# Second layer normalisation of a fused block moved from VectorE to ScalarE, its shift and the output's shift to GpSimd

## The chip, the cores and the metric

The kernel runs on one NeuronCore of a Trainium2 chip. The metric is the device time of one execution in microseconds, as a median over runs.

## What is computed

The input is `x` of 8 batches, 1024 rows and 512 columns in fp32. One block of attention kind and one feed-forward block follow each other, each inside two layer normalisations:

```python
x = x + _layernorm(attn(_layernorm(x)))
x = x + _layernorm(ffn(_layernorm(x)))

# attn(x): s = sigmoid(silu(x @ s_w1 + s_b1) @ s_w2.T + s_b2); u = (x @ B_w.T + B_b) * s
#   h_t = h_(t-1) @ A.T + u_t over the 1024 rows;  y = h @ C_w.T + C_b + x @ D_w.T + D_b
#   returns y * sigmoid(x @ g_w.T + g_b)
# ffn(x): sq_relu(x @ Ws1) @ Ws2 + a routed part, whose weight trunc(softmax(top2)) is 0
#   except where it is exactly 1
# _layernorm(x) = (x - mean) / sqrt(var + 1e-05) over the last axis
```

## The kernel before

A batch is 8 tiles (`L = 8`) of 128 rows, in two halves of `MS = 4`. TensorE does every product three times over (`mm3`, L416 to L418) with operands split in a high and a low part, since the high part alone would be too coarse. The order of the instructions of each engine is written out by hand, in two functions with the same names on each engine: `tail_and_scan` (the gates 0 to 3 of batch b and the 12 steps of its state scan, mixed with the end of batch b-1's feed-forward) and `body` (the rest of batch b up to its first half of the feed-forward, mixed with the first normalisation and projections of batch b+1). Batch 0 and batch 7 are written out, and batches 1 to 6 are six passes of one hardware loop on each engine. Engines wait for each other by counting semaphores alone, and each engine works through its queue in the order written.

The names that matter here, for tile `j`:

- `attn(j)`, `attn_norm(j)` on VectorE: product with the gate, its statistics, the normalisation. `x1(j)` on GpSimd (L1480) adds the input and gives `xres`, the input of the second block.
- `x1_stats(j)` on VectorE (L1039, L1040, L1095): mean and variance of `xres` in `mvx`, `rsx`. `x1_rs(j)` on GpSimd (L1456): `rsx` to the power -1/2. `x1_norm(j)` on VectorE (L1099): `work = (xres - mean) * rsx`. `T(j)` on TensorE (L479) transposes `work`. `t_hi(j)` on ScalarE (L817) and `t_low(j)` on VectorE (L1103) split the result.
- `W1f(m,f)`, `hidden(m,f)` (L834, L836), `h2(m,f)` (L1148), `h2_low(m,f)` on GpSimd (L1495) make the hidden layer of half `m`. `R(m)`, `lg(m)` on ScalarE (L842), `RT(m)` (L527), `top(m)` make the router's values. `W2(j)` gives the result `z` of tile `j` in a PSUM bank.
- `z_stats(j)` on VectorE (L1165), `z_rs(j)` on GpSimd (L1456), `z_shift(j)` on VectorE (L1170, one column: `nmz = -mean * rsz`), `zn(j)` on ScalarE (L861: `work = z * rsz + nmz`), `outs(j)` on GpSimd (L1484) adds `xres`. `zn(j)` also frees the bank: three banks, `TM`, go round in a ring, and by its order `W2(7)` takes over the bank of `zn(5)`, and `Y(0)`, the first output product of the next stage (L467), that of `zn(6)`.
- `H(m,f)`, `sig`, `h1(m,f)` (L1119, L1125), `h1_low(m,f)` on GpSimd (L1489) and `SG(m)` (L578 to L581) belong to the next batch's state gate. `SG` needs both `h1_low` of its half.
- `scan_add(i)` on VectorE (L1062, L1065, L1068) adds the result of scan step `i` (L436, L442, L447). The next step on TensorE waits for it.

GpSimd's part of `body` sets the order in which these small steps pass it:

```python
for j in range(1, L):
    v_rs(b, j)
    if j == 5 and prep:
        h1_low(b + 1, 0, 0)
    x1_rs(b, j - 1)
    ...
    x1(b, j)
```

Of the kernel before, what the change touches and what calls it, by code (L numbers as in the profile page):

```python
# [5 lines left out]
ALU = mybir.AluOpType  # L6
# [6 lines left out]
P = 128  # L13
# [3 lines left out]
def build(nc, x, A, AT, BwT, Bb, CwT, Cb, DwT, Db, s1T, s1b, s2T, s2b, gwT, gb, Ws1, Ws2, W1, W2, Wr, eye, out):  # L17
# [17 lines left out]
    with ExitStack() as ctx:  # L35
        def sb(name, shape, dt=F32):
            return ctx.enter_context(nc.sbuf_tensor(name, shape, dt))
# [5 lines left out]
        def pair(name, cols):  # L43
# [47 lines left out]
        mvx = sb("mvx", [P, L, 2])  # L91
        rsx = sb("rsx", [P, L])
        mvz = sb("mvz", [P, L, 2])
        rsz = sb("rsz", [P, L])
# [18 lines left out]
                    z_var=L, z_nm=L, top_ok=NM,  # L113
                    v_rs=L, x1_ok=L, x1_rs=L, h2lo_ok=NM * KF, z_rs=L, out_ok=L,
                    xres_ld0=16, xres_ld1=16, x1_st0=16, x1_st1=16, out_st0=16, out_st1=16)
# [6 lines left out]
        w_ld = {n: sem("ld_" + n) for n in ("a", "comb", "small", "s1", "b", "s2", "bias", "g", "d", "c", "f1", "f2", "r")}  # L122
        chain = sem("dve_chain")
        hi_ok = sem("weights_hi")
        lo_dve = sem("weights_lo_dve")
# [653 lines left out]
        def _(eng):  # L779
# [30 lines left out]
            def t_hi(b, rep, j):  # L810
# [75 lines left out]
            def body(b, rep):  # L886
                a = (b, rep)
                prep = rep + 1 < NB
                hs(*a, 2)
                gate(*a, 4)  # L890
                hs(*a, 3)
                gate(*a, 5)
                if prep:
                    ft_hi(*a, 0)
                hs(*a, 4)
                t_hi(*a, 0)
                gate(*a, 6)
                if prep:
                    ft_hi(*a, 1)
                hs(*a, 5)  # L900
                t_hi(*a, 1)
                gate(*a, 7)
                if prep:
                    ft_hi(*a, 2)
                hs(*a, 6)
                if prep:
                    ft_hi(*a, 3)
                hs(*a, 7)
                t_hi(*a, 2)
                if prep:  # L910
                    sig(*a, 0, 0)
                    sig(*a, 0, 1)
                t_hi(*a, 3)
                if prep:
                    ft_hi(*a, 4)
                    s_gate(*a, 0)
                    ft_hi(*a, 5)
                hidden(*a, 0, 0)
                if prep:
                    ft_hi(*a, 6)  # L920
                if prep:
                    hidden(*a, 0, 1)
                    ft_hi(*a, 7)
                    lg(*a, 0)
                    t_hi(*a, 4)
                    zn(*a, 0)
                    t_hi(*a, 5)
                    zn(*a, 1)
                    sig(*a, 1, 0)
                    t_hi(*a, 6)  # L930
                    zn(*a, 2)
                    sig(*a, 1, 1)
                    zn(*a, 3)
                    t_hi(*a, 7)
                    s_gate(*a, 1)
                else:
                    hidden(*a, 0, 1)
                    lg(*a, 0)
                    t_hi(*a, 4)
                    t_hi(*a, 5)  # L940
                    t_hi(*a, 6)
                    zn(*a, 0)
                    t_hi(*a, 7)
                    zn(*a, 1)
                    zn(*a, 2)
# [85 lines left out]
        def _(eng):  # L1031
# [64 lines left out]

            def x1_norm(b, rep, j):
                eng.wait_ge(S["x1_rs"], body_at("x1_rs", b, j))
                eng.tensor_scalar(work[:, j, :], xres[:, j, :], mvx[:, j, 0:1], rsx[:, j:j + 1],  # L1099
                                  ALU.subtract, ALU.mult).then_inc(S["xn2_ok"], 1)  # L1100

            def low_of(dst, bank, hi):
# [63 lines left out]

            def z_shift(b, rep, j):
                i = b + shift(f"z{j}")
                eng.wait_ge(S["z_rs"], body_at("z_rs", i, j))
                eng.scalar_tensor_tensor(out=nmz[:, j:j + 1], in0=mvz[:, j, 0:1], scalar=-1.0, in1=rsz[:, j:j + 1],  # L1170
                                         op0=ALU.mult, op1=ALU.mult).then_inc(S["z_nm"], 1)

            def tail_and_scan(b, rep):
# [24 lines left out]
                if prep:  # L1198
                    ln1_stats(b + 1, 4)
                if tail:  # L1200
                    z_shift(*a, 4)
# [14 lines left out]
                if tail:  # L1216
                    z_shift(*a, 6)
                    z_stats(*a, 7)
                if prep:
                    ln1_stats(b + 1, 6)  # L1220
                if tail:
                    z_shift(*a, 7)
                if prep:
                    ln1_stats(b + 1, 7)
# [6 lines left out]
            def body(b, rep):  # L1231
# [8 lines left out]
                attn_norm(*a, 1)  # L1240
                x1_norm(*a, 0)
                if prep:
# [4 lines left out]
                attn_norm(*a, 2)  # L1247
                x1_norm(*a, 1)
                t_low(*a, 0)
# [6 lines left out]
                attn_norm(*a, 3)  # L1256
                x1_norm(*a, 2)
                t_low(*a, 1)
# [8 lines left out]
                attn_norm(*a, 4)  # L1267
                x1_norm(*a, 3)
                if prep:
# [9 lines left out]
                attn_norm(*a, 5)  # L1279
                x1_norm(*a, 4)  # L1280
                if prep:
# [7 lines left out]
                attn_norm(*a, 6)  # L1289
                x1_norm(*a, 5)  # L1290
                if prep:
# [7 lines left out]
                attn_norm(*a, 7)  # L1299
                x1_norm(*a, 6)  # L1300
                if prep:
                    ft_low(*a, 7)
                if prep:
                    x1_stats(*a, 7)
                    t_low(*a, 4)
                    z_stats(*a, 0)
                    z_stats(*a, 1)
                    z_shift(*a, 0)
                    x1_norm(*a, 7)
                    z_shift(*a, 1)  # L1310
# [5 lines left out]
                    z_shift(*a, 2)  # L1316
                    z_stats(*a, 3)
                    h1(*a, 1, 1)
                    z_shift(*a, 3)
                    t_low(*a, 7)  # L1320
                    u_of(*a, 1)
                else:
                    t_low(*a, 4)
                    x1_stats(*a, 7)
                    t_low(*a, 5)
                    x1_norm(*a, 7)
                    z_stats(*a, 0)
                    t_low(*a, 6)
                    z_shift(*a, 0)
                    z_stats(*a, 1)  # L1330
                    t_low(*a, 7)
                    z_shift(*a, 1)
                    top(*a, 0)
                    z_stats(*a, 2)
                    z_shift(*a, 2)
                    z_stats(*a, 3)
# [49 lines left out]
            h2(NB, NB, 1, 0)  # L1386
            z_shift(NB - 1, NB - 1, 3)
            h2(NB, NB, 1, 1)
            top(NB, NB, 1)
            eng.memset(flag[:, 1:2], 0.0).then_inc(chain_end, 1)  # L1390
            for j in range(MS, L):
                z_stats(NB, NB, j)
                if j > MS:
                    z_shift(NB, NB, j - 1)

# [7 lines left out]
            eng.tensor_reduce(flag[:, 0:1], dif[:, :], AX.X, ALU.max).then_inc(flag_dve, 1)  # L1403
            z_shift(NB, NB, L - 1)
            for j in (L - 2, L - 1):
# [42 lines left out]
        def _(eng):  # L1448
# [153 lines left out]
```

## Time and profile before

| what | value |
|---|---|
| device time, 3 runs | 1006.11, 1006.33, 1007.48 us (median 1006.33) |
| span of the profiled execution, first to last instruction | 1001.7 us |
| mean granted TensorE clock | 0.984 |
| TensorE busy (matmuls) | 939.3 us, 94% |
| VectorE busy | 693.4 us, 69% |
| ScalarE busy | 269.8 us, 27% |
| GpSimd busy | 400.9 us, 40% |

The profiled execution's own time is known as its span alone, and the runs' median stands 4.6 us above it. Busy time of TensorE is modelled from the starts of its matmuls: in an undisturbed stretch a matmul of 512 columns is shown with 0.39 us and the next starts 0.23 us after it, so that a row's idle time is some 0.16 us less than what the wait really cost. In the rows below, PE is TensorE, PEld its weight loads, DVE VectorE, ACT ScalarE, POOL GpSimd. "Idle before" is how long the engine did nothing before the row, and the name behind the arrow is what ended it.

### The profile page before, as it was taken

How to read it: one execution, taken by the hardware profiler on the slowest of the kernel's cores; microseconds unless marked ns; L12 is line 12 of the kernel's file. 1: busy time of each engine (PE TensorE's matmuls, PEld its weight loads, DVE VectorE, ACT ScalarE, POOL GpSimd, SP SyncE). 2: the span in 40 equal slices, each digit the busy share in tenths (PEclk: the TensorE clock that was granted, in tenths of full speed). 3: DMA queues.
4: the chain of work that ended last, by engine and by line, in shares of the span. 5: the costliest groups of instructions: out<-in, count | busy, mean ns of one | idle time of the engine just before them, and what ended most of it. 6: DMA issues, size and time to landing. Idle time of an engine off the chain costs nothing. (4 is left out here: it accounts for less than half of the span.)

```text
span 1001.7 us, 13829 instructions
## 1 busy us (share of the span) xinstructions
PE 939.3 (94%) x4496; PEld 765.9 (76%) x4496; DVE 693.4 (69%) x1552; ACT 269.8 (27%) x487; POOL 400.9 (40%) x413
## 2 busy tenths in 40 slices
PE   5799999999999999999999999999999999999894
PEld 4678888788777887778777888778887788788673
DVE  5637875788737886478856887478873788636774
ACT  4321232222322223222232223222232222222122
POOL 2353443434514345143543444343451434524353
PEclk9799999999999999999999999999999999999997
DMA  7220114010142101321031211401014210212112
GB/s 266 84 85 1 43 43 168 35 66 27 43 168 84 42 0 67 143 84 42 22 145 44 84 42 42 168 31 65 29 42 168 84 42 0 83 43 85 43 43 85
DMA packets 14592, 72.21 MB, mean 72 GB/s; under 512 B 2374, under 2 KB 4550, under 8 KB 6476
## 3 DMA queue, kind: packets, MB, share of 16 engines
q1 hardware_dynamic: 14540, 71.67, 18.9%
q14 instruction: 38, 0.31, 0.1%
q8 instruction: 14, 0.23, 0.1%
HBM read 38.11 MB, written 33.55 MB: 72 GB/s over the span
## 5 line engine op out<-in xcount | busy, mean ns | idle before, releaser
L1456 POOL TENSOR_TENSOR rsv<-rsv,negh 128x1 f32<-128x1 f32 x64 | 35.8, 560 | 198.0 <-DVE rsv L1085 198.0
L416 PE MATMUL TM<-gw_hi,xT_hi 128*128 128x512 f32 x256 | 102.6, 401 | 0.0
L1099 DVE TENSOR_SCALAR work<-xres,mvx,rsx 128x512 f32<-128x512 f32 x64 | 88.3, 1380 | 17.8 <-POOL rsx L1456 17.7
L418 PE MATMUL TM<-dw_hi,xT_lo 128*128 128x512 f32 x256 | 100.6, 393 | 0.0
L418 PE MATMUL TM<-gw_hi,xT_lo 128*128 128x512 f32 x256 | 100.5, 393 | 0.0
L417 PE MATMUL TM<-gw_lo,xT_hi 128*128 128x512 f32 x256 | 100.4, 392 | 0.0
L417 PE MATMUL TM<-dw_lo,xT_hi 128*128 128x512 f32 x256 | 100.1, 391 | 0.0
L416 PE MATMUL TM<-dw_hi,xT_hi 128*128 128x512 f32 x256 | 100.0, 390 | 0.0
L861 ACT ACTIVATE work<-TM,nmz,rsz 128x512 f32<-128x512 f32 x62 | 48.2, 778 | 188.9 <-DVE nmz L1170 188.9
L1495 POOL TENSOR_TENSOR h_lo<-hf,h_hi 128x512 fp32r<-128x512 f32 x32 | 43.0, 1343 | 116.3 <-DVE h_hi L1148 116.3
L1484 POOL TENSOR_TENSOR work<-work,xres 128x512 f32<-128x512 f32 x62 | 80.0, 1291 | 20.9 <-ACT work L861 20.7
L1480 POOL TENSOR_TENSOR xres<-work,xres 128x512 f32<-128x512 f32 x64 | 84.9, 1327 | 5.8 <-DVE work L1089 5.8
L799 ACT ACTIVATE work<-TM 128x512 f32<-128x512 f32 x64 | 38.2, 597 | 177.2 <-PE TM L418 104.9
L1456 POOL TENSOR_TENSOR rsz<-rsz,negh 128x1 f32<-128x1 f32 x64 | 37.3, 583 | 106.8 <-DVE rsz L1165 106.8
L1456 POOL TENSOR_TENSOR rsx<-rsx,negh 128x1 f32<-128x1 f32 x64 | 44.1, 689 | 63.0 <-DVE rsx L1095 63.0
L1489 POOL TENSOR_TENSOR h_lo<-hf,h_hi 128x512 fp32r<-128x512 f32 x32 | 43.3, 1352 | 49.5 <-DVE h_hi L1125 49.4
L416 PE MATMUL TM<-f2w_hi,h_hi 128*128 128x512 f32 x124 | 54.6, 440 | 6.8 <-ACT work L861 6.8
L1170 DVE SCALAR_TENSOR_TENSOR nmz<-mvz,rsz 128x1 f32<-128x1 f32 x64 | 49.5, 774 | 12.3 <-POOL rsz L1456 8.4
L1081 DVE TENSOR_TENSOR work<-TM,work 128x512 f32<-128x512 f32 x64 | 44.0, 688 | 18.7 <-PE TM L418 18.7
L417 PEld LDWEIGHTS TM<-dw_lo,xT_hi 128*128 128x128 f32 x256 | 48.1, 188 | 10.6
L418 PEld LDWEIGHTS TM<-gw_hi,xT_lo 128*128 128x128 f32 x256 | 48.1, 188 | 10.4
L418 PEld LDWEIGHTS TM<-dw_hi,xT_lo 128*128 128x128 f32 x256 | 48.1, 188 | 10.3
(165 smaller groups left out, 2325.4 us busy)
## 6 DMA issues: line engine op xcount, KB each, us to landing
xin<-in_x SPq DMA_DIRECT2D x16, 1024.0 KB, 7.5
xres<-in_x SPq DMA_DIRECT2D x16, 1024.0 KB, 7.0
x_scratch<-xres SPq DMA_DIRECT2D x16, 1024.0 KB, 3.9
out<-work SPq DMA_DIRECT2D x15, 1024.0 KB, 4.8
xres<-in_g_w_t SPq DMA_DIRECT2D x1, 1024.0 KB, 8.9
xres<-in_D_w_t SPq DMA_DIRECT2D x1, 1024.0 KB, 10.9
work<-in_Ws SPq DMA_DIRECT2D x2, 512.0 KB, 9.5
out<-work SPq DMA_DIRECT2D x4, 256.0 KB, 2.0
```

The lines of the kernel that those rows point to most:

```text
L416: eng.matmul(ps, lhs[0], rhs[0], start=first, stop=False)
L417: eng.matmul(ps, lhs[0], rhs[1], start=False, stop=False)
L418: return eng.matmul(ps, lhs[1], rhs[0], start=False, stop=last)
L861: eng.activation(work[:, j, :], z_bank(rep, j)[:, :], ACT.Identity, bias=nmz[:, j:j + 1], scale=rsz[:, j:j + 1]).then_inc(S["zn_ok"], 1)
L1081: eng.tensor_tensor(work[:, j, :], tm_bank(f"y{j}")[:, :], work[:, j, :], ALU.mult)\
L1099: eng.tensor_scalar(work[:, j, :], xres[:, j, :], mvx[:, j, 0:1], rsx[:, j:j + 1], ALU.subtract, ALU.mult).then_inc(S["xn2_ok"], 1)
L1170: eng.scalar_tensor_tensor(out=nmz[:, j:j + 1], in0=mvz[:, j, 0:1], scalar=-1.0, in1=rsz[:, j:j + 1], op0=ALU.mult, op1=ALU.mult).then_inc ...
L1456: return eng.tensor_tensor(dst, src, negh[:, 0:n], ALU.pow)
L1480: eng.tensor_tensor(xres[:, j, :], work[:, j, :], xres[:, j, :], ALU.add).then_inc(S["x1_ok"], 1)
L1484: eng.tensor_tensor(work[:, j, :], work[:, j, :], xres[:, j, :], ALU.add).then_inc(S["out_ok"], 1)
L1489: eng.tensor_tensor(h1_lo[:, f, :], hf_row(name), h1_hi[:, f, :].bitcast(F32), ALU.subtract).then_inc(S["h1lo_ok"], 1)
L1495: eng.tensor_tensor(h2_lo[:, f, :], hf_row(name), h2_hi[:, f, :].bitcast(F32), ALU.subtract).then_inc(S["h2lo_ok"], 1)
```

## The change

`x1_norm(j)` leaves VectorE's queue and becomes one ScalarE activation, `work = xres * rsx + nmx`. The column `nmx = -mean * rsx` is new. It and `nmz` are each made by GpSimd in one `tensor_scalar` on 128x1 right behind the power, with a wait of GpSimd for its own power in between (`link`: a semaphore raised by the power, waited for, and lowered again). `z_shift` leaves VectorE.

```diff
+            def x1_norm(b, rep, j):
+                eng.wait_ge(S["x1_nm"], body_at("x1_nm", b, j))
+                eng.activation(work[:, j, :], xres[:, j, :], ACT.Identity, bias=nmx[:, j:j + 1], scale=rsx[:, j:j + 1])\
+                   .then_inc(S["xn2_ok"], 1)
...
-            def x1_norm(b, rep, j):
-                eng.wait_ge(S["x1_rs"], body_at("x1_rs", b, j))
-                eng.tensor_scalar(work[:, j, :], xres[:, j, :], mvx[:, j, 0:1], rsx[:, j:j + 1],
-                                  ALU.subtract, ALU.mult).then_inc(S["xn2_ok"], 1)
-
...
-            def z_shift(b, rep, j):
-                i = b + shift(f"z{j}")
-                eng.wait_ge(S["z_rs"], body_at("z_rs", i, j))
-                eng.scalar_tensor_tensor(out=nmz[:, j:j + 1], in0=mvz[:, j, 0:1], scalar=-1.0, in1=rsz[:, j:j + 1],
-                                         op0=ALU.mult, op1=ALU.mult).then_inc(S["z_nm"], 1)
-
...
+            def link(ins):
+
+                ins.then_inc(pool_chain, 1)
+                eng.wait_ge(pool_chain, 1)
+                eng.sem_inc(pool_chain, -1)
+
+            def minus_shift(dst, mean, rs):
+
+                return eng.tensor_scalar(dst, mean, rs, -1.0, ALU.mult, ALU.mult)
+
...
             def x1_rs(b, j):
                 eng.wait_ge(S["x1_var"], body_at("x1_var", b, j))
-                power(rsx[:, j:j + 1], rsx[:, j:j + 1], 1).then_inc(S["x1_rs"], 1)
+                link(power(rsx[:, j:j + 1], rsx[:, j:j + 1], 1))
+                minus_shift(nmx[:, j:j + 1], mvx[:, j, 0:1], rsx[:, j:j + 1]).then_inc(S["x1_nm"], 1)
 
             def z_rs(b, j):
                 eng.wait_ge(S["z_var"], body_at("z_var", b, j))
-                power(rsz[:, j:j + 1], rsz[:, j:j + 1], 1).then_inc(S["z_rs"], 1)
+                link(power(rsz[:, j:j + 1], rsz[:, j:j + 1], 1))
+                minus_shift(nmz[:, j:j + 1], mvz[:, j, 0:1], rsz[:, j:j + 1]).then_inc(S["z_nm"], 1)
```

In ScalarE's `body`, `x1_norm(6)` comes between `hidden(0,1)`/`ft_hi(7)` and `lg(0)`, and in the last batch `x1_norm(7)` comes between `t_hi(4)` and `t_hi(5)`:

```diff
                     hidden(*a, 0, 1)
                     ft_hi(*a, 7)
+                    x1_norm(*a, 6)
                     lg(*a, 0)
                     t_hi(*a, 4)
                     zn(*a, 0)
                     t_hi(*a, 5)
+                    x1_norm(*a, 7)
                     zn(*a, 1)
...
                 else:
                     hidden(*a, 0, 1)
+                    x1_norm(*a, 6)
                     lg(*a, 0)
                     t_hi(*a, 4)
+                    x1_norm(*a, 7)
                     t_hi(*a, 5)
                     t_hi(*a, 6)
                     zn(*a, 0)
```

The hardware loop over the batches moves in VectorE's instruction stream as well. Before, the branch with which the loop begins is row 205 of VectorE's listing (ISA and REGISTER_ALU are register instructions, L1381 is the loop's line, `carry` and `u` belong to the scan):

```order
L1381 UNCONDITIONAL_BRANCH
L1381 ISA
L1061 ISA
L1062 TENSOR_TENSOR carry<-SC,u 128x128
L1057 REGISTER_ALU
L1065 TENSOR_TENSOR carry<-SC,carry 128x127
L1057 REGISTER_ALU
L1065 TENSOR_TENSOR carry<-SC,carry 128x124
```

With the change the branch is row 193:

```order
L1364 UNCONDITIONAL_BRANCH
L1364 ISA
L1079 ISA
L1080 TENSOR_TENSOR carry<-SC,u 128x128
L1075 REGISTER_ALU
L1083 TENSOR_TENSOR carry<-SC,carry 128x127
L1075 REGISTER_ALU
L1083 TENSOR_TENSOR carry<-SC,carry 128x124
L1155 ISA
L1158 REGISTER_ALU
L1161 CAST h_hi<-hf 128x512
L1062 ISA
```

The same instructions follow the branch, and they stand 12 instructions nearer to the start of the stream: 8 `x1_norm` and 4 `z_shift` of batch 0 are gone from in front of them.

On GpSimd, the end of the part for batch 0 is, before (L1456 is the power, `rsz` the variance of the output, L1484 `outs`, L1489 `h1_low`):

```order
L1456 TENSOR_TENSOR rsz<-rsz,negh 128x1 x2
L1484 TENSOR_TENSOR work<-work,xres 128x512
L1489 TENSOR_TENSOR h_lo<-hf,h_hi 128x512
L1456 TENSOR_TENSOR rsz<-rsz,negh 128x1
L1484 TENSOR_TENSOR work<-work,xres 128x512 x2
L1456 TENSOR_TENSOR rsz<-rsz,negh 128x1
L1489 TENSOR_TENSOR h_lo<-hf,h_hi 128x512
```

and with the change:

```order
L1475 TENSOR_TENSOR work<-work,xres 128x512
L1480 TENSOR_TENSOR h_lo<-hf,h_hi 128x512
L1435 TENSOR_TENSOR rsz<-rsz,negh 128x1
L1445 TENSOR_SCALAR nmz<-mvz,rsz 128x1
L1475 TENSOR_TENSOR work<-work,xres 128x512 x2
L1435 TENSOR_TENSOR rsz<-rsz,negh 128x1
L1445 TENSOR_SCALAR nmz<-mvz,rsz 128x1
L1480 TENSOR_TENSOR h_lo<-hf,h_hi 128x512
```

Each power is followed by its shift, and `h1_low(1,1)` in the last row has two of them more in front of it.

## Rows read from the trace of the kernel before

**Rows 1.** Window of one loop pass: length, busy us by engine, clock, DMA share.

```profile
397.05:515.69 118.64, 114.70 (x558) 93.65 (x557) 85.24 (x192) 31.47 (x57) 47.90 (x51) 1.00 0.18 71
```

**Rows 2.** Waits of TensorE: us in total, times, longest.

```profile
PE SC L442 <- DVE carry L1065: 7.4, 5, 1.8
PE TM L416 <- ACT work L861: 6.8, 8, 1.3
...
PE FM L581 <- POOL h_lo L1489: 4.6, 13, 0.4
PE TM L467 <- ACT work L861: 3.5, 6, 0.6
```

**Rows 3.** Timeline around `zn(5)`, with `W2(7)` last: start, duration.

```profile
305.14 0.55 POOL L1456 TENSOR_TENSOR rsz<-rsz,negh 128x1 f32<-128x1 f32 x1 [3.35 <-DVE rsz L1165]
305.65 1.26 POOL L1484 TENSOR_TENSOR work<-work,xres 128x512 f32<-128x512 f32 x1
305.72 1.21 DVE L1170 SCALAR_TENSOR_TENSOR nmz<-mvz,rsz 128x1 f32<-128x1 f32 x1 [0.41 <-POOL rsz L1456]
306.96 0.78 ACT L861 ACTIVATE work<-TM,nmz,rsz 128x512 f32<-128x512 f32 x1 [2.14 <-DVE nmz L1170]
307.79 0.50 PE L416 MATMUL TM<-f2w_hi,h_hi 128*128 128x512 f32 x1 [0.77 <-ACT work L861]
```

**Rows 4.** The same for `zn(6)` and `Y(0)`.

```profile
309.58 0.55 POOL L1456 TENSOR_TENSOR rsz<-rsz,negh 128x1 f32<-128x1 f32 x1 [2.67 <-DVE rsz L1165]
312.42 0.78 ACT L861 ACTIVATE work<-TM,nmz,rsz 128x512 f32<-128x512 f32 x1 [4.29 <-DVE nmz L1170]
313.25 0.50 PE L467 MATMUL TM<-bias_y,ones 128*128 128x512 f32 x1 [0.57 <-ACT work L861]
```

**Rows 5.** Where the loop jumps back: timeline, waits, window, fetches in a pass.

```profile
401.61 0.29 DVE L1062 TENSOR_TENSOR carry<-SC,u 128x128 f32<-128x128 f32 x1 [2.79 <-PE SC L436]
406.49 0.29 DVE L1065 TENSOR_TENSOR carry<-SC,carry 128x127 f32<-128x127 f32 x1 [4.59 <-issue]
406.84 0.93 PE L442 MATMUL SC<-carry,apt 128*128 128x124 f32 x6 [1.18 <-DVE carry L1065]
DVE carry L1065 <- issue: 24.4, 5, 5.2
287.20:290.50 3.30, 3.30 (x11) 2.62 (x10) 1.40 (x4) 0.00 (x0) 1.28 (x1) 0.50 0.66 273
q14 instruction: 5, 0.04, 0.1%
```

**Rows 6.** Groups (busy us, mean ns); the shift's min/median/max; waits on VectorE itself.

```profile
L1099 DVE TENSOR_SCALAR work<-xres,mvx,rsx 128x512 f32<-128x512 f32 x64 | 88.3, 1380 | 17.8 <-POOL rsx L1456 17.7
L1170 DVE SCALAR_TENSOR_TENSOR nmz<-mvz,rsz 128x1 f32<-128x1 f32 x64 | 49.5, 774 | 12.3 <-POOL rsz L1456 8.4
L186 POOL TENSOR_TENSOR f2w_hi<-lgt,f2w_hi 128x32 fp32r<-128x32 f32 x1 | 0.2, 250 | 0.0
L1170 DVE SCALAR_TENSOR_TENSOR nmz<-mvz,rsz x64: 147/1053/1287, 147.5 to 994.4; 128x1 f32<-128x1 f32 x64
DVE rsv L1085 <- DVEq L1036: 4.9, 31, 0.2
```

**Rows 7.** The wait in `SG(0)`.

```profile
361.12 0.50 PE L581 MATMUL FM<-h_lo,s2w_hi 128*128 128x512 f32 x1 [0.34 <-POOL h_lo L1489]
```

**Rows 8.** Around `lg(0)` and `RT(0)`.

```profile
376.19 0.54 POOL L1456 TENSOR_TENSOR rsx<-rsx,negh 128x1 f32<-128x1 f32 x1 [1.34 <-DVE rsx L1095]
377.64 0.59 ACT L842 ACTIVATE hf<-FM 16x512 f32<-16x512 f32 x1 [0.53 <-PE FM L518]
```

**Rows 9.** Batch 7 on TensorE, and GpSimd's last instruction.

```profile
947.54 0.47 PE L416 MATMUL FM<-x2T_hi,f1w_hi 128*128 128x512 f32 x1 [2.61 <-issue]
980.63 1.87 PE L527 MATMUL FM<-comb,hf 16*128 16x8 f32 x8 [3.13 <-ACT hf L842]
999.76 0.38 POOL L1568 PARTITION_ALL_REDUCE flag<-flag  x1 [5.96 <-issue]
```

More of the change, by code:

```diff
@@ L92, in build @@
         rsx = sb("rsx", [P, L])
+        nmx = sb("nmx", [P, L])
         mvz = sb("mvz", [P, L, 2])
@@ L113, in build @@
                     z_var=L, z_nm=L, top_ok=NM,
-                    v_rs=L, x1_ok=L, x1_rs=L, h2lo_ok=NM * KF, z_rs=L, out_ok=L,
+                    v_rs=L, x1_ok=L, x1_nm=L, h2lo_ok=NM * KF, out_ok=L,
                     xres_ld0=16, xres_ld1=16, x1_st0=16, x1_st1=16, out_st0=16, out_st1=16)
@@ L123, in build @@
         chain = sem("dve_chain")
+        pool_chain = sem("pool_chain")
         hi_ok = sem("weights_hi")
@@ L894, in body @@
                     ft_hi(*a, 0)
+                x1_norm(*a, 0)
                 hs(*a, 4)
@@ L899, in body @@
                     ft_hi(*a, 1)
+                x1_norm(*a, 1)
                 hs(*a, 5)
@@ L904, in body @@
                     ft_hi(*a, 2)
+                x1_norm(*a, 2)
                 hs(*a, 6)
@@ L909, in body @@
                 t_hi(*a, 2)
+                x1_norm(*a, 3)
                 if prep:
@@ L916, in body @@
                     s_gate(*a, 0)
+                x1_norm(*a, 4)
+                if prep:
                     ft_hi(*a, 5)
                 hidden(*a, 0, 0)
+                x1_norm(*a, 5)
                 if prep:
@@ L1199, in tail_and_scan @@
                     ln1_stats(b + 1, 4)
-                if tail:
-                    z_shift(*a, 4)
                 scan_add(*a, 8)
@@ L1205, in tail_and_scan @@
                 scan_add(*a, 9)
-                if tail:
-                    z_shift(*a, 5)
                 scan_add(*a, 10)
@@ L1216, in tail_and_scan @@
                 if tail:
-                    z_shift(*a, 6)
                     z_stats(*a, 7)
@@ L1220, in tail_and_scan @@
                     ln1_stats(b + 1, 6)
-                if tail:
-                    z_shift(*a, 7)
-                if prep:
                     ln1_stats(b + 1, 7)
@@ L1240, in body @@
                 attn_norm(*a, 1)
-                x1_norm(*a, 0)
                 if prep:
@@ L1247, in body @@
                 attn_norm(*a, 2)
-                x1_norm(*a, 1)
                 t_low(*a, 0)
@@ L1256, in body @@
                 attn_norm(*a, 3)
-                x1_norm(*a, 2)
                 t_low(*a, 1)
@@ L1267, in body @@
                 attn_norm(*a, 4)
-                x1_norm(*a, 3)
                 if prep:
@@ L1279, in body @@
                 attn_norm(*a, 5)
-                x1_norm(*a, 4)
                 if prep:
@@ L1289, in body @@
                 attn_norm(*a, 6)
-                x1_norm(*a, 5)
                 if prep:
@@ L1299, in body @@
                 attn_norm(*a, 7)
-                x1_norm(*a, 6)
                 if prep:
@@ L1307, in body @@
                     z_stats(*a, 1)
-                    z_shift(*a, 0)
-                    x1_norm(*a, 7)
-                    z_shift(*a, 1)
                     t_low(*a, 5)
@@ L1325, in body @@
                     t_low(*a, 5)
-                    x1_norm(*a, 7)
                     z_stats(*a, 0)
                     t_low(*a, 6)
-                    z_shift(*a, 0)
                     z_stats(*a, 1)
                     t_low(*a, 7)
-                    z_shift(*a, 1)
                     top(*a, 0)
                     z_stats(*a, 2)
-                    z_shift(*a, 2)
                     z_stats(*a, 3)
@@ L1386, in _ @@
             h2(NB, NB, 1, 0)
-            z_shift(NB - 1, NB - 1, 3)
             h2(NB, NB, 1, 1)
@@ L1392, in _ @@
                 z_stats(NB, NB, j)
-                if j > MS:
-                    z_shift(NB, NB, j - 1)
             eng.wait_ge(exp_ok, 1)
@@ L1403, in _ @@
             eng.tensor_reduce(flag[:, 0:1], dif[:, :], AX.X, ALU.max).then_inc(flag_dve, 1)
-            z_shift(NB, NB, L - 1)
             for j in (L - 2, L - 1):
```

2 lines of the change are left out of this document (removed).

## Prediction, before the change was run

> **What bounds the kernel.** I read first the window of one loop pass, then who waits for whom on TensorE, then the timeline at each of those waits. In a pass TensorE is busy for 114.7 of 118.6 us, VectorE for 85.2, GpSimd for 47.9 and ScalarE for 31.5 [rows 1]. TensorE is the bound, and what the change is worth is what it takes off TensorE's waits; VectorE's 69% is worth nothing by itself. Two kinds of TensorE's waits end in work that the change touches, and two more end in VectorE or in GpSimd's short instructions [rows 2]. Each matmul row hides 0.16 us of its wait (it is shown 0.39 us long and the next starts 0.23 us later), so I add that to each.
>
> **What the change removes.** VectorE loses 64 normalisations of 1.38 us and 64 one-column shifts of 0.77 us, 138 us in all [rows 6]. Both are as long as they are because they wait for GpSimd: the shift at 305.72 starts 0.07 us behind a GpSimd sum of 1.26 us and ends with it [rows 3]. The Trainium skill (SBUF — State Buffer, Who interferes with whom) says that VectorE and GpSimd take a shared pair of ports as an exclusive lock and the later one blocks for the whole instruction; the trace agrees with its 1.21 us.
>
> **What it adds.** ScalarE gets 64 activations. The nearest row is its own `zn` from PSUM, 0.78 us [rows 3]; 64 of these are 50 us, 6 a pass on an engine that is busy 31.5 of 118.6. GpSimd gets 128 times a wait for its own power and a shift. No row shows it. From below: a two-input instruction on 32 columns takes 0.25 us there; from above: the power on one column, 0.55 [rows 3]. The wait for itself costs VectorE 4.9 / 31 = 0.16 us [rows 6]. A power is no plain arithmetic, so I take the lower row, 0.2 + 0.15 = 0.35 us, with bounds of 0.15 (the wait alone) and 0.75. The Trainium skill speaks against the move (GPSIMD Engine Reference, its comparison of elementwise work): VectorE remains the place for elementwise work, GpSimd being 1.96 times slower in an addition of 2048 columns. By it the shift would cost 0.3 us (an estimate: 1.96 times the 0.147 of VectorE's quickest), and the sum would be 1 to 3 us smaller.
>
> **Step by step on TensorE.**
>
> 1. `W2(7)` waits for `zn(5)` 0.77 us [rows 3]. Power done at 305.69; the shift in VectorE ends at 306.93. Now it ends at 306.05, `zn(5)` at 306.85, and TensorE, which was ready at 307.79 - 0.77 = 307.02, waits for nothing. Wait and shift are hidden here up to 307.02 - 306.85 + 0.35 = 0.5 us. Seven times 0.77 + 0.1 (the matmuls ahead are short): **+6.1**.
> 2. `Y(0)` waits for `zn(6)` 0.57 us [rows 4]. The power is done at 310.13 and `zn(6)` starts only at 312.42, since VectorE's shift stands in its queue and then behind GpSimd. Now it starts near 310.5. Six times 0.58 + 0.16: **+4.5**.
> 3. At the loop's jump back VectorE runs the first addition of the scan at 401.61 and the second only at 406.49, 4.59 us idle with nothing that the profile names but issue; TensorE then waits 1.18 us for it. This happens in each of the 5 jumps (24.4 us of VectorE, 7.4 of TensorE) [rows 2, 5]. In the same pass 5 packets of instructions are fetched, 8 KB each [rows 5], while the loop is 327 instructions of the built program long. I read this so: the code of the loop's start is no longer held; a block is fetched, its last few instructions run, and the next block is asked for only then and takes 5 us, beside the batch's loads and the store of the output. The loop's start stands three instructions before a block's end. With the change 12 instructions in front of it are gone, so blocks at fixed places end 15 instructions into the loop: behind both early additions, the cast of `h2` and the first statistics. VectorE gets there near 408, when the block (406.4) has come. TensorE's wait goes: 7.4 + 5 x 0.16 = 8.2. After the longest of them (1.8 us) the clock granted is 0.50 for 3.3 us [rows 5], its 1.2 GHz level, which costs another 1.7. **+9.9**. If blocks don't stand so, 0.
> 4. `SG(0)` waits 0.34 us for `h1_low(0,1)` [rows 7]. VectorE comes to `h1(0,0)` and `h1(0,1)` about 1.4 us sooner without `x1_norm(3)` (mean in rows 6), and GpSimd with it. Six times 0.34 + 0.16: **+3.0**. The other seven waits of that group [rows 2] are `SG(1)` for `h1_low(1,1)`, but this one now has two more shifts before it on GpSimd (0.7 us), against a `zn(2)`, and an `outs(2)` behind it, that come about 1 us sooner as in step 1: **0**, with -3 and +4 as ends.
> 5. `lg(0)` on ScalarE runs at 377.64, and `x1_norm(6)` now stands before it. Its power ends at 376.73 [rows 8], the shift at 377.1, so it runs until 377.9. `RT(0)` comes 0.25 us later, seven times: **-1.8**. The other normalisations sit in ScalarE's idle times of 2 to 4 us ahead of work that waits for TensorE, and cost nothing; were that cover gone, 0.8 us each.
> 6. Batch 7. `W1f(0,0)` waits 2.61 us for `t_low(3)` [rows 9], which stands behind three `x1_norm` on VectorE; that wait goes, with 0.4 of `T(3)`: +3.2. Then ScalarE has `x1_norm(7)` before `t_hi(5)`, and VectorE's `t_low(5)` and `z_stats(0)` wait for it: -2. `RT(1)` waits 3.13 us [rows 9] for ScalarE, where `zn(2)` and `zn(3)` come 1.2 us sooner each and let `hidden` go: +3 to +4. At the end GpSimd has four shifts more in its queue ahead of its last instruction (999.76) [rows 9], and nothing more is won. **+5**, ends 2 and 8.
>
> The sum is 26.7 us. The profiled span is 1001.7, so its forecast is 975; to the runs' median, 4.6 us above it, it is 1006.3 - 26.7 = **980 us**.
>
> **Rivals.**
>
> - The wait at the jump stays, or moves to another place on the path (the first fetch is made longer by stores that now start 1 us sooner). For it: it hangs on where blocks end, which only one kernel shows. Against it: the same place in 5 of 5 jumps. Sum without step 3: 16.8, **990 us** (1006.3 - 16.8 = 989.5). The Trainium skill (Runtime: NRT & Kernel Launch, Instruction fetch mechanics) has a rule: a taken branch whose target is not in the window of two pages makes the sequencer wait for a fetch. By that rule a fetch remains at each jump; the trace agrees in that, and what I expect to go is only the second one behind it.
> - GpSimd's wait and shift cost 0.7 us rather than 0.35. Then `zn(5)` misses by 0.2, `SG(1)` loses twice the surplus, `RT(0)` once: five times 0.35 in a pass, over seven passes 12 us. **992 us**.
> - Slower than before, by one mechanism: waiting for its own power empties GpSimd each time, and wait and shift cost more than 0.43 + 26.7 / 35 = 1.2 us (35 times a surplus counts, above). At 1.3 us it is **1010 us**. For it: 16 of them a pass on the queue that TensorE waits for at `SG`. Against it: VectorE does the same to itself with 0.16 us [rows 6].
> - No change: the gains at `zn` are eaten by ScalarE, because a normalisation blocks its queue before `hs` or `t_hi`. By the timeline the nearest of these has 1 us to spare. **1006 us**.
>
> **Chances.** Forecast 0.60 (973 to 986), wait at the jump stays 0.18 (986 to 994), dear shift 0.13 (988 to 1004), no change 0.04, slower 0.04; the rest lies below 973. The range from 972 to 994 leaves out the dearer half of the third case, the last two and little else. A difference of 0.2% (2 us) is about what a measurement of this kernel can tell from none: faster 0.92, same 0.03, slower 0.05.
>
> **What would show it.** Steps 1 and 2: no idle time of TensorE ahead of `W2(7)` and `Y(0)`. Step 3: the second addition of the scan follows the first within 2 us, and the issue wait stands at another line of VectorE, or nowhere. Step 4: none ahead of `SG(0)`. Step 5: a wait of `RT(0)` near 0.5 us. GpSimd's new group shows its mean directly. VectorE falls to about 555 us, ScalarE rises to 320. I am wrong if TensorE shows a new wait that none of these names, above all for ScalarE's transposes' copies, or if the issue wait of VectorE is still at the second addition.

## The result and the profile after

The changed kernel takes 977.5 us (median of 4 runs, 976.37 to 978.54) against 1006.22 (median of 4) for the kernel before: ratio 0.9734, 95% interval 0.9705 to 0.9762, 28.7 us less by the medians and 26.8 by the ratio. Run again beside other kernels it took 978.12 against 1003.59, ratio 0.9756 (0.9736 to 0.9776), 25.5 us less by the medians. Forecast were 980.0 us and 26.7 us less.

The page of the changed kernel, its busy time by engine and the granted clock in 40 slices:

```profile
span 976.8 us, 14021 instructions
PE 931.5 (95%) x4496; PEld 766.7 (78%) x4496; DVE 566.6 (58%) x1424; ACT 321.1 (33%) x551; POOL 437.4 (45%) x541
PEclk9899999999999999999999999999999999999997
```

One pass of the loop by the windows view, the partner of [rows 1]:

```profile
391.04:506.17 115.13, 113.79 (x558) 93.89 (x557) 69.14 (x177) 37.92 (x64) 52.59 (x66) 1.00 0.19 73
```

A pass is 3.5 us shorter. TensorE is idle for 1.3 us of it where it was for 3.9, and the rest of a wait, which a matmul's row hides, fell with it. VectorE lost 16 us of work a pass. TensorE's waits, the partner of [rows 2], without two that belong to the start of the kernel (us in total, times, longest):

```profile
PE FM L529 <- ACT hf L849: 6.4, 9, 2.0
PE FM L583 <- POOL h_lo L1480: 2.7, 7, 0.4
PE TM L418 <- ACT work L868: 2.5, 1, 2.5
PE SC L444 <- DVE carry L1080: 1.9, 5, 0.4
PE TR L481 <- ACT work L824: 1.7, 1, 1.7
```

The wait of 7.4 for the second scan addition is gone, and so are the wait for `zn` at the bias product of `Y(0)` (3.5) and seven of the eight at L416 (6.8), which is L418 now. The eighth, `W2(3)` of the last batch, was 1.3 us and is 2.5. `SG` waits in 7 places instead of 13. The first scan addition, shown late in two jumps before (0.7 in all), is late in five (1.9). L529 is `RT`, behind ScalarE's copy `lg` (L849). It waited before the change too:

```profile
PE FM L527 <- ACT hf L842: 4.8, 8, 3.1
```

`RT(1)` of the last batch fell from 3.1 to 2.0, `RT(0)` of batches 0 to 6 rose from 0.24 to 0.55 each, and `RT(0)` of the last batch, which did not wait before, now waits 0.56.

The new instructions, the partner of [rows 6]: one row each of the groups of GpSimd and of ScalarE, the view of the line of the shifts (min/median/max in ns), and GpSimd's wait for itself:

```profile
L1435 POOL TENSOR_TENSOR rsx<-rsx,negh 128x1 f32<-128x1 f32 x64 | 44.8, 699 | 64.2 <-DVE rsx L1113 64.2
```

```profile
L824 ACT ACTIVATE work<-xres,nmx,rsx 128x512 f32<-128x512 f32 x64 | 52.1, 815 | 33.4 <-POOL nmx L1445 32.5
```

```profile
L1445 POOL TENSOR_SCALAR nmx<-mvx,rsx x64: 262/265/587, 92.9 to 939.3; 128x1 f32<-128x1 f32 x64
L1445 POOL TENSOR_SCALAR nmz<-mvz,rsz x64: 264/265/322, 147.8 to 968.4; 128x1 f32<-128x1 f32 x64
```

```profile
POOL nmz L1445 <- POOLq L1441: 13.2, 64, 0.2
```

A shift on one column takes 0.265 us, and GpSimd's wait for its own power 13.2 / 64 = 0.21 us. Together 0.47 us where I had put 0.35. Around `zn(5)` and `W2(7)`, where [rows 3] had 1.27 us from the end of the power to the start of `zn(5)`, the timeline now reads:

```profile
300.75 0.55 POOL L1435 TENSOR_TENSOR rsz<-rsz,negh 128x1 f32<-128x1 f32 x1 [2.88 <-DVE rsz L1178]
...
301.50 0.26 POOL L1445 TENSOR_SCALAR nmz<-mvz,rsz 128x1 f32<-128x1 f32 x1 [0.21 <-POOLq L1441]
...
301.80 0.78 ACT L868 ACTIVATE work<-TM,nmz,rsz 128x512 f32<-128x512 f32 x1 [1.37 <-POOL nmz L1445]
...
302.63 0.49 PE L418 MATMUL TM<-f2w_hi,h_hi 128*128 128x512 f32 x1
```

From the power's end (301.30) to `zn(5)` it is 0.50 us. `zn(5)` ends at 302.58, and `W2(7)` starts at 302.63 without a wait, just behind `RT(1)`: in time by a few hundredths. At the jump back of the loop, the partner of [rows 5]: the timeline, VectorE's wait for issue, and the queue of instructions in the pass:

```profile
395.05 0.29 DVE L1080 TENSOR_TENSOR carry<-SC,u 128x128 f32<-128x128 f32 x1 [3.35 <-PE SC L438]
...
395.40 0.93 PE L444 MATMUL SC<-carry,apt 128*128 128x127 f32 x6 [0.38 <-DVE carry L1080]
...
396.37 0.29 DVE L1083 TENSOR_TENSOR carry<-SC,carry 128x127 f32<-128x127 f32 x1 [1.02 <-PE SC L444]
```

```profile
DVE hs_lo L1092 <- issue: 1.9, 6, 0.3
```

```profile
q14 instruction: 5, 0.04, 0.1%
```

The second addition (396.37) waits for TensorE's product and no longer for its own issue. Of VectorE's waits for issue 1.9 us are left at L1092 and 1.5 at L1057 (6 times each, the longest 0.3). The pass still fetches five packets of instructions.

### The profile page after: what moved, and what is told of

Its sections match the earlier page's. It is cut to its first block and busy times, and to the rows that moved or that the text cites. A ratio compares the mean times of both kernels' runs of the same rounds, so it can differ in the third digit from the quotient of the medians.

```text
span 976.8 us, 14021 instructions
## 1 busy us (share of the span) xinstructions
PE 931.5 (95%) x4496; PEld 766.7 (78%) x4496; DVE 566.6 (58%) x1424; ACT 321.1 (33%) x551; POOL 437.4 (45%) x541
## 5 line engine op out<-in xcount | busy, mean ns | idle before, releaser
L418 PE MATMUL TM<-gw_hi,xT_hi 128*128 128x512 f32 x256 | 102.5, 400 | 0.0
L418 PE MATMUL TM<-dw_hi,xT_hi 128*128 128x512 f32 x256 | 99.7, 389 | 0.0
L824 ACT ACTIVATE work<-xres,nmx,rsx 128x512 f32<-128x512 f32 x64 | 52.1, 815 | 33.4 <-POOL nmx L1445 32.5
L1116 DVE TENSOR_TENSOR x2T_lo<-TR,x2T_hi 128x512 fp32r<-128x512 f32 x64 | 43.8, 685 | 26.4 <-ACT x2T_hi L819 26.4
L418 PE MATMUL TM<-f2w_hi,h_hi 128*128 128x512 f32 x124 | 54.1, 436 | 2.9 <-ACT work L868 2.5
```

The lines of the kernel that those rows point to most:

```text
L418: eng.matmul(ps, lhs[0], rhs[0], start=first, stop=False)
L824: eng.activation(work[:, j, :], xres[:, j, :], ACT.Identity, bias=nmx[:, j:j + 1], scale=rsx[:, j:j + 1])\
L1116: return eng.tensor_tensor(dst, bank[:, :].rearrange("p (k n) -> p k n", n=P), hi.bitcast(F32), ALU.subtract)
```

## Experiments

Each is compared with the kernel before on the same chip, whose median was 1003.23 us (first four), 1002.32 (next four) or 1003.59 (last three). "Memsets" are one-column writes to a tensor that nothing reads, at the start of VectorE's stream, before its first wait. They cost TensorE nothing there (in experiment 1 the first `RT(0)` starts at 141.0 us, in the kernel before at 141.4) and only push VectorE's loop along in its instruction stream.

**1. The kernel before, with its loop moved on by 16 instructions.**

```diff
+        spare = sb("spare", [P, 32])
...
+            for i in range(16):
+                eng.memset(spare[:, i:i + 1], 0.0)
```

> The kernel before, with 16 one-column memsets of a spare tensor ahead of VectorE's first wait for its input. They do no work that counts and only move VectorE's hardware loop 16 instructions on, from 3 instructions before a block's end to 13 behind a block's start. Theory A (step 3: the wait at the jump back is for a block of instructions whose end falls three instructions into the loop): TensorE's wait for the second addition of the scan goes, and as 13 + 327 instructions now fit in three blocks, the fetches of a pass may go too; 994 to 997 us. Theory B (the wait at the jump has to do with how loaded VectorE or the DMA queues are, and the change took it away by making VectorE's queue shorter): nothing changes, 1004 to 1008 us.

991.98 us, ratio 0.9882 (0.9853 to 0.9911): 11.2 us less, although the kernel computes all as before and 16 instructions more. TensorE's waits:

```profile
PE TM L417 <- ACT work L862: 6.8, 8, 1.4
...
PE FM L582 <- POOL h_lo L1492: 4.8, 14, 0.4
...
PE TM L468 <- ACT work L862: 3.5, 6, 0.6
```

Those for `zn` (6.8 and 3.5) and `SG` stand as in [rows 2], within 0.2 us; the one for `carry` is gone. One pass by the windows view, and the only queue that its DMA view lists:

```profile
378.90:495.50 116.60, 114.30 (x558) 93.71 (x557) 85.47 (x194) 31.48 (x56) 47.73 (x50) 1.00 0.19 72
```

```profile
q1 hardware_dynamic: 1159, 8.45, 18.7%
```

The pass has no packet of the instruction queue at all. From the `RT(0)` of batch 1 to that of batch 6 it takes 583.1 us instead of 595.0, and before and after that stretch the two traces differ by less than 1 us. So the waits at the jump are VectorE's instruction fetches, and where the loop lies decides them.

**2. The change with the loop put back to its old place** (the same edit with 12 memsets).

> The changed kernel, with 12 one-column memsets of a spare tensor ahead of VectorE's first wait, so that its loop starts at the same place of a block as before the change. Theory A: the wait of 1.2 to 1.8 us for the second addition comes back in each of the 5 jumps, 985 to 988 us. Theory B: 976 to 979 us.

985.75 us, ratio 0.9818 (0.9790 to 0.9846). The wait that the change had removed is there again, in TensorE's waits and in VectorE's:

```profile
PE SC L445 <- DVE carry L1084: 7.0, 5, 1.7
```

```profile
DVE carry L1084 <- issue: 24.0, 5, 5.1
```

The change of work alone gives 17.5 us. The shift of the loop is the rest: by the ratios 0.0062 (second run of the changed kernel) to 0.0084 (first), 6 to 8 us. The traces agree: the same stretch from `RT(0)` to `RT(0)` takes 584.0 us here and 575.6 in the changed kernel.

**3. The change with a loop that is never fetched again** (the same edit with 20 memsets).

> The changed kernel with 20 such memsets: VectorE's loop of 311 instructions starts 5 behind a block's start and lies in three blocks. Theory A, with room for four blocks: no instruction fetch in a pass and no wait at the jump, TensorE's 0.55 us at the first addition goes five times, 974 to 975.5 us. Theory A with room for two or three blocks: the first fetch of a pass stays, 977 us. Theory B: 977.5 us.

981.42 us, ratio 0.9778 (0.9748 to 0.9808), by the ratios 2 to 4 us slower than the changed kernel, and 6 above what was expected. The waits for both additions are gone, as they should be, and the trace has no packet on q14, the queue of the five packets, between 269 and 870 us. But around `RT(0)` the timeline shows:

```profile
482.82 0.34 POOL L1448 TENSOR_SCALAR nmx<-mvx,rsx 128x1 f32<-128x1 f32 x1 [0.21 <-POOLq L1444]
...
483.20 0.81 ACT L825 ACTIVATE work<-xres,nmx,rsx 128x512 f32<-128x512 f32 x1 [0.59 <-POOL nmx L1448]
...
483.92 0.57 ACT L850 ACTIVATE hf<-FM 16x512 f32<-16x512 f32 x1
...
484.55 1.05 PE L530 MATMUL FM<-comb,hf 16*128 16x8 f32 x8 [1.00 <-ACT hf L850]
```

and the windows view right behind it, the clock being the third number from the end:

```profile
485.90:489.30 3.40, 3.40 (x10) 2.65 (x9) 2.22 (x6) 0.00 (x0) 0.81 (x2) 0.52 0.75 308
717.70:721.10 3.40, 3.40 (x10) 2.62 (x9) 2.24 (x7) 0.00 (x0) 0.95 (x3) 0.53 0.75 308
834.00:837.40 3.40, 3.40 (x9) 2.62 (x9) 2.20 (x5) 0.00 (x0) 0.81 (x2) 0.51 0.75 308
```

The power ahead of this shift took 0.81 us, where the changed kernel has 0.54 at the same place, and the shift 0.34 instead of 0.27. ScalarE stands still 0.59 us for it, `lg(0)` is queued behind that, and `RT(0)` starts 1.0 us late. In six passes this happens each time, and in three the clock then is granted at 1.2 GHz instead of 2.4 for 3.4 us. Such a pass took 116.6 us, one without it 115.0. In the changed kernel itself the same `RT(0)` is late by some 0.5 us (it starts 0.82 us after the matmul ahead of it, here 1.28), and no such window follows in any pass. Memsets don't touch ScalarE; that this place is the cause was a guess until experiment 6.

**4. The output's part alone** (`z_shift` to GpSimd, `x1_norm` stays; 4 memsets keep the loop in its old place). Of the diff of the change it has `link`, `minus_shift`, the new `z_rs` and the end of `z_shift`, and not the rest.

> Of the change only the output's part: GpSimd makes the shift for zn, while x1_norm stays on VectorE; 4 memsets keep VectorE's loop at its old place in a block. My theory: TensorE's waits for zn(5) and zn(6) go (steps 1 and 2, 10.6 us) and 2 to 4 us in batch 7, while the wait at the jump stays; 990 to 994 us. Rival (VectorE's load made the waits, and x1_norm, 88 of its 138 us, is what mattered): less than 5 us of gain, over 1001 us.

990.2 us, ratio 0.9856 (0.9826 to 0.9885), 13.0 us less by the medians and 14.4 by the ratio. No wait for `zn` in a pass is left. `SG` still waits in 13 places and the second addition in 5:

```profile
PE SC L444 <- DVE carry L1067: 7.7, 5, 1.8
...
PE FM L583 <- POOL h_lo L1480: 4.7, 13, 0.4
```

**5. The second normalisation's part alone** (`x1_norm` to ScalarE, `z_shift` stays; 8 memsets keep the place).

> The second normalisation alone moved (x1_norm and its shift to ScalarE and GpSimd; z_shift stays on VectorE), with 8 one-column memsets ahead so that VectorE's loop lies in its instruction blocks as before. My theory: the waits for zn(5), zn(6) and the wait at the jump belong to the output's shift and to the block layout, so they stay (20 us of the 24.5 that the whole change gave), and what this part gives is SG(0) 3 us and little more, less RT(0), which now waits for hf behind x1_norm(6) (-2): 1001 to 1005 us against about 1005 of before. Rival: most of the gain comes from VectorE's 128x512 work leaving it (0.54 us x 64), so this part alone gives 8 us or more: 990 to 997 us.

999.26 us, ratio 0.9961 (0.9946 to 0.9976), 3 to 4 us less. The 88 us of VectorE's work that it moves are thus worth about an eighth of the whole. In TensorE's waits, `zn` and the second addition have stayed, and in the passes only `SG(0)` has gone:

```profile
PE TM L419 <- ACT work L869: 7.7, 8, 2.2
...
PE SC L445 <- DVE carry L1084: 7.0, 5, 1.7
...
PE FM L584 <- POOL h_lo L1507: 2.1, 7, 0.3
```

**6. Experiment 3 with `lg(0)` first in the pass.**

```diff
                     ft_hi(*a, 7)
-                    x1_norm(*a, 6)
                     lg(*a, 0)
+                    x1_norm(*a, 6)
                     t_hi(*a, 4)
```

> The kernel of the 20-memset run, with ScalarE's copy for the router's logits, lg(0), ahead of x1_norm(6) in the pass. In that run x1_norm(6) waited 0.6 us for its shift, lg(0) stood behind it, RT(0) on TensorE started 1.28 us after the matmul ahead of it instead of 0.82, and in three passes of six the granted clock then fell to half for 3.4 us. Theory: that late RT(0) is what costs the half clock; with lg(0) first RT(0) starts about 0.5 us after the matmul ahead, the clock stays at full speed in all passes, each pass takes about 114.3 us, and the time is 971 to 975 us. Rival: the half clock comes from a denser TensorE as a whole and not from this wait: it still falls in the middle of passes, and the time stays at 978 to 982 us.

971.42 us, ratio 0.9687 (0.9667 to 0.9707). `RT(0)` starts 0.51 us after the matmul ahead of it:

```profile
481.22 0.59 ACT L850 ACTIVATE hf<-FM 16x512 f32<-16x512 f32 x1 [0.53 <-PE FM L521]
...
481.71 0.80 ACT L825 ACTIVATE work<-xres,nmx,rsx 128x512 f32<-128x512 f32 x1
...
481.86 1.05 PE L530 MATMUL FM<-comb,hf 16*128 16x8 f32 x8 [0.24 <-ACT hf L850]
```

and no window at half clock is left between 50 and 949 us. Against experiment 3 the ratios differ by 0.0091, 9 us: 6 x 0.77 + 0.3 = 4.9 are the wait itself, 3 x 1.6 = 4.8 the clock, and `SG(1)`'s wait grew by 0.8 in all. That settles where the 6 us of experiment 3 were lost; why power and shift take longer there than in the changed kernel stays open.

**7. As 6, and in the last batch too `lg(0)` first, and `x1_norm(7)` behind `t_hi(5)`.**

```diff
                 else:
                     hidden(*a, 0, 1)
-                    x1_norm(*a, 6)
                     lg(*a, 0)
+                    x1_norm(*a, 6)
                     t_hi(*a, 4)
-                    x1_norm(*a, 7)
                     t_hi(*a, 5)
+                    x1_norm(*a, 7)
```

> The kernel of the run before, and in the last batch too lg(0) ahead of x1_norm(6), and x1_norm(7) behind t_hi(5). The step of my forecast on batch 7 says that x1_norm(7) ahead of t_hi(5) gives 2 us back (the trace after shows 2.5 us of W2(3) waiting there, and 1.7 us of T(3)). Theory: 2 to 3.5 us less than the run before, 968.5 to 972.5 us. Rival: the tail is bound by the chain of VectorE's and GpSimd's work behind it, and the end moves by less than 1 us.

972.09 us, ratio 0.9688 (0.9668 to 0.9709): no gain. The wait at `W2(3)` did fall, from 2.5 us to 0.8, but `RT(1)` then waited 2.7 instead of 2.0, and the clock behind it was at half for 6.7 us instead of 3.4. Windows of this kernel, then of experiment 6:

```profile
948.90:955.60 6.70, 6.64 (x19) 5.32 (x20) 2.42 (x11) 1.97 (x3) 2.81 (x4) 0.51 0.39 159
```

```profile
949.40:952.80 3.40, 3.08 (x8) 2.46 (x8) 1.39 (x8) 1.53 (x2) 1.52 (x2) 0.54 0.36 147
```

The rival holds: what is won at one wait of the last batch is paid at the next, and in clock.

**8. As 7, and GpSimd's `h1_low(1,1)` ahead of `z_rs(3)`, ScalarE's `zn(3)` behind `t_hi(7)` and `s_gate(1)`.**

```diff
+                if prep:
+                    h1_low(b + 1, 1, 1)
                 z_rs(b, 3)
                 if prep:
-                    h1_low(b + 1, 1, 1)
                     outs(b, 3)
...
-                    zn(*a, 3)
                     t_hi(*a, 7)
                     s_gate(*a, 1)
+                    zn(*a, 3)
```

> The kernel of the run before, with GpSimd's h1_low(1,1) ahead of z_rs(3), and on ScalarE zn(3) behind t_hi(7) and s_gate(1): power and shift of z_rs(3) (about 1.4 us) no longer stand ahead of the low half that SG(1) waits for (0.55 us in each of 7 passes after the change). Theory: SG(1)'s wait goes and nothing else comes late, 3 to 4 us less than the run before: 965 to 969 us. Rival: the output's normalisations of the tail (zn(4) to zn(6)) come later by zn(3)'s delay and TensorE waits for them at W2(7) or Y(0) as before the change: no gain or a loss of up to 5 us.

966.69 us, ratio 0.9642 (0.9617 to 0.9668), 5 us less than experiment 7 and the fastest kernel here. No matmul of `SG(1)` waits any longer (a weight load ahead of it stands idle 0.19 us), and `zn(5)` and `zn(6)` still come in time.

**9. The changed kernel again.**

> The changed kernel once more, as the ground for the other runs on this chip: 975 to 980 us.

978.12 us, as expected.

**10. The changed kernel, without memsets, with `lg(0)` first in the pass.**

> The changed kernel without any memsets, with ScalarE's lg(0) ahead of x1_norm(6) in the pass. It differs from the fastest form of the 20-memset series (971.4 us) in the block layout of VectorE's instructions alone. Theory: RT(0)'s wait of 0.82 us falls to about 0.5 in 7 passes, 2 us off; and the first scan addition still waits 0.55 us for VectorE's fetch in 5 passes, so 2.7 us of fetch are left against the 20-memset form: 974 to 976 us. Rival: the fetches cost nothing at their new place, and this kernel reaches 970 to 972 us.

974.07 us, ratio 0.9711 (0.9691 to 0.9730). The fetch of VectorE's instructions at its new place still costs about 2.5 us against experiment 6. Of the 4 us that this gives against the changed kernel, seven times 0.31 = 2.2 are `RT(0)`. The first addition shows what the fetch still costs:

```profile
PE SC L444 <- DVE carry L1080: 2.0, 5, 0.4
```

**11. The changed kernel with each shift computed twice** (0.48 us more in each of 128 chains; same output).

```diff
-                minus_shift(nmx[:, j:j + 1], mvx[:, j, 0:1], rsx[:, j:j + 1]).then_inc(S["x1_nm"], 1)
+                link(minus_shift(nmx[:, j:j + 1], mvx[:, j, 0:1], rsx[:, j:j + 1]))
+                minus_shift(nmx[:, j:j + 1], mvx[:, j, 0:1], rsx[:, j:j + 1]).then_inc(S["x1_nm"], 1)
```

> The changed kernel with every shift computed twice on GpSimd, each with its wait for the one before: 0.48 to 0.55 us more in each of 128 chains from statistics to normalisation, nothing else changed. Theory (the shift's price is hidden except where the chain of GpSimd is already what TensorE waits for): the low half h1_low(1,1) for SG(1) comes about 1 us later in 7 passes, lg(0) behind x1_norm(6) 0.5 us later in 7 passes, the last batch 1 to 2 us more, and zn(5) and zn(6) still come in time: 10 to 14 us more than the changed kernel, 987 to 991 us. Rival (all hidden): at most 3 us more. Rival (the whole chain is dear, as in my forecast's case of a shift above 1.2 us): zn(5) and zn(6) wait again too, above 1000 us.

1000.77 us, ratio 0.9967 (0.9945 to 0.9989): 22.7 us more than the changed kernel, half as much again as I had expected at most, and in the range of the rival that calls the whole chain dear. TensorE's waits and two windows:

```profile
PE FM L529 <- ACT hf L849: 11.1, 9, 2.9
PE FM L583 <- POOL h_lo L1482: 9.1, 7, 1.3
...
PE TM L418 <- ACT work L868: 5.1, 8, 1.8
```

```profile
496.30:499.70 3.40, 3.40 (x11) 2.55 (x10) 1.88 (x6) 0.00 (x0) 1.76 (x5) 0.57 0.75 311
732.00:735.40 3.40, 3.40 (x10) 2.53 (x10) 1.85 (x6) 0.00 (x0) 1.89 (x5) 0.54 0.73 299
```

`RT` waits 4.7 us more, `SG(1)` 6.4, and the row of `zn` 2.6: `zn(5)` is back with seven waits of 0.47, while `W2(3)` of the last batch fell from 2.5 to 1.8. Together that is 13.7. Of the rival's two waits only `zn(5)` has come back; for `zn(6)` TensorE does not wait. What I left out is the clock. `RT(0)` is late by 1.28 us from one matmul to the next as in experiment 3, and behind it, in batches 0 to 6, three windows at half clock appear. The last batch has two such windows and one of 6.8 us, where the changed kernel has one of 3.4. TensorE is shown 938.8 us busy instead of 931.5, 7.3 more. This kernel's runs spread with the clock: the fastest, with a mean granted clock of 0.986, took 994.81 us, the slowest, with 0.979, 1004.37.

## Why the prediction was right

**Steps 1 and 2** (waits for `zn(5)` and `zn(6)`, 6.1 + 4.5). Right: both waits are gone, and experiment 4, which moves only the output's shift, gives 13.0 us. What that has over 10.6 is only in part located. In its trace `RT(1)` of the last batch waits 2.0 us instead of 3.13, and the clock there is at half for 3.4 us instead of 6.8, worth 1.7. But there is a window of 3.4 us at half clock at 936.8 that the kernel before doesn't have, and it takes the 1.7 back. The shift's price of 0.35 us was the term that was mis-sized: it is 0.47. The cover of 0.5 us that I worked out in step 1 was just wide enough for it. Experiment 11 shows how narrow it is: with 0.48 us more, `zn(5)` makes TensorE wait 0.47.

**Step 3** (the jump, 9.9). Right in mechanism, and the step on which the forecast stood or fell; its size in the change was put some 2 to 4 us too high. Experiment 1 has it alone: 11.2 us with not one instruction of the computation moved. In the change it is worth 6 to 8 us (experiment 2). Two things make up the difference. The fetch at the jump itself stays, as forecast, but it delays the first addition at five jumps by 0.55 us from start to start, 2.7 in all, where the kernel before lost 0.2 to 0.6 a jump, 1.6 in all; the forecast had no term for these 1.1 us. And the 1.7 us of clock stand for one window that followed a wait of 1.8 us; experiment 2, with waits up to 1.7 at the same place, and experiment 4, with one of 1.8, have no such window in a pass. Experiments 1 and 6 are free of the late first addition too, which fits that experiment 1 gained more than the forecast's 9.9.

**Step 4** (`SG(0)` 3.0, `SG(1)` 0). Right: 13 waits became 7, and experiment 5 shows that it is `x1_norm` leaving VectorE that frees `SG(0)`. `SG(1)` kept its 0.39 us, and experiment 8 got it by order alone.

**Step 5** (`RT(0)`, -1.8). Right: 0.31 us in each of seven, -2.2 (0.51 us from the matmul ahead of it became 0.82). The eighth, in the last batch, went from 0.20 to 0.83, which the forecast left out. The step's size hides its weight. The order `x1_norm(6)` before `lg(0)` is the change's weakest place: a little later still and it takes the clock with it (experiments 3 and 11). Undoing it in the changed kernel's passes gives 4 us (experiment 10), and the waits of `RT` fall from 6.5 to 2.9 us. Of that, 2.2 are the seven `RT(0)`. The other 1.3 are `RT(1)` of the last batch, whose order the experiment leaves alone: there a window at half clock lies at 944.0, ahead of `RT(1)`, and TensorE comes to it later. Experiment 2 has the same (952.9, `RT(1)` 0.7) with the old order, so this part is the clock's doing.

**Step 6** (batch 7, +5). The directions are as forecast, and one size is not. The wait of `W1f(0,0)` is gone, and `T(3)` waits 0.2 us less: 3.0 against 3.2. `x1_norm(7)` before `t_hi(5)` costs: `W2(3)` waited before too and rose by 1.15 us, and `RT(0)` now waits 0.56, 1.7 against 2. But `RT(1)`, which was to bring 3 to 4, waits only 1.1 less, and the wait at L517 (1.07) went with it, 2.2 in all. What fills the gap is luck: the clock around `RT(1)` is at half for 3.4 us where it was 6.8 before, worth 1.7, and the forecast had no term for it. From the `RT(0)` of batch 6 on, TensorE's last matmul ends 5.4 us sooner, 0.9 of them step 1's; then the kernel takes 12.3 us to its end instead of 11.5. So the batch gave 3.7 instead of 5. Two lines of the kernel before, then the timeline of the changed kernel there, and the window behind `RT(1)`:

```profile
967.18 0.50 PE L416 MATMUL TM<-f2w_hi,h_hi 128*128 128x512 f32 x1 [1.34 <-ACT work L861]
...
975.37 0.50 PE L517 MATMUL FM<-x2T_hi,f2w_hi 128*128 128x512 f32 x1 [1.07 <-ACT hf L834]
```

```profile
939.61 0.82 ACT L824 ACTIVATE work<-xres,nmx,rsx 128x512 f32<-128x512 f32 x1 [3.36 <-POOL nmx L1445]
...
944.83 0.50 PE L418 MATMUL TM<-f2w_hi,h_hi 128*128 128x512 f32 x1 [2.49 <-ACT work L868]
...
955.80 1.05 PE L529 MATMUL FM<-comb,hf 16*128 16x8 f32 x8 [2.00 <-ACT hf L849]
```

```profile
957.30:960.70 3.40, 3.40 (x9) 2.67 (x10) 1.77 (x8) 1.54 (x2) 1.01 (x1) 0.53 0.48 195
```

**The sum.** Without step 3 I had 16.8 us; experiment 2 has 17.5, and its two halves 13.0 and 3.1, 16.1. By the ratios these are 18.3, 14.4 and 3.9, and the halves add up to the whole. So the work without the jump gave 0.7 to 1.5 us more than forecast, although step 6 was put 1.3 too high: some 2 to 3 us came where no term stands. 1.7 of them may be the window at half clock of the kernel before at 287.2, which experiment 2 lacks as well; the rest was not traced. The sum came out closer than its terms, and that part is luck. **The rivals.** The wait at the jump did not stay, nor did "no change" or "slower" come. The dear shift (0.7 us, 12 us more than my sum) did not come. Its slope was 35 times a surplus, five a pass, though the losses it names (0.2 + 0.7 + 0.35) come to 1.25 us a pass and not to 1.75. Experiment 11 has a surplus of 0.48 us, and a batch of it shows which losses are real: `SG(1)` 0.9, twice the surplus, `RT(0)` 0.46 and `zn(5)` 0.47, once each, `zn(6)` none. Four times seven times 0.48 is 13.4, against 13.7 measured in waits; the rest of the 22.7 is mostly the clock. By the slope of 35 the measured 0.47 us should have lost 4 us against 0.35, but the cover took it: nothing at `zn(5)` and `SG(1)`, and 0.06 more than forecast at each `RT(0)`. **The busy times.** VectorE has 566.6 us (about 555 forecast), ScalarE 321.1 (320).

The Trainium skill (GPSIMD Engine Reference, comparison of elementwise work) keeps elementwise work on VectorE and gives 1.96 as the ratio of an addition of 2048 columns. The estimate that the prediction worked out from that for a shift on GpSimd, 0.3 us, was near: the trace has 0.265, and the wait of GpSimd for its own power adds 0.21. Yet the move paid, since the shift left a queue in which it had waited.

## What to carry to other kernels

Read first which of the critical engine's waits end in the work that moves: here 64 one-column shifts were worth about four times as much as 64 normalisations of 128x512. Before crediting a change to the work it moves, shift the loop of the engine that sees issue waits by a few idle instructions; if the time changes by as much, the gain is one of layout and can be had alone. And when a moved instruction waits for a slow neighbour, look at what is queued behind it in the same engine: a copy of 0.6 us before eight small matmuls cost the clock as well, in three passes of six. A window at half clock costs 1.7 us here, and it follows the same wait in one kernel and not in its neighbour. Compare the clock of a stage before crediting a difference of that size to an edit.

## What was not expected of the hardware

- A loop of 311 to 327 instructions on VectorE was fetched again in each pass, or not at all, by its place alone: five packets of 8 KB a pass in the kernel before and in the changed one, none in experiments 1 and 3. In experiment 1, 16 idle instructions were worth 11.2 us.
- The clock fell to half for 3.4 us, or twice that, behind `RT`: eight short matmuls whose first one came late. It did so in three of six passes with 1.28 us from the matmul ahead (experiment 3), in none with 0.82 or 0.51 (the changed kernel, experiment 6), and for 6.7 us behind a wait of 2.7 (experiment 7). Experiment 11 had 1.28 in batches 0 to 6 and the drop in three of the seven. Other waits are no surer sign: one of 2.5 us at `W2(3)` of the last batch is followed by half clock in experiments 2, 3 and 10, and not in the changed kernel or experiment 6, and the same 2.7 us before `RT(1)` brought 3.4 us of it in experiment 5 and 6.7 in experiment 7. In one pass of experiment 5 it fell at 778.0 us, behind the 0.79 us before `W2(7)` that brought none in the kernel before. Why is open.
- GpSimd's own power on one column took 0.55 us in the rows above, 0.81 at one place of experiment 3, and 0.70 on average in the group of `rsx`. With the shift and the wait the chain on GpSimd is 1.0 to 1.2 us, and more than half of it is the power.
